# A decoder layer on one core: per-head scores on 32 rows of the array, and projections without a bias product

## The reference

```
x = x + attn(layernorm(x))        # 16 heads of 32, rope on q and k, causal, bias on q, k, v and on the output
x = x + xattn(layernorm(x), ctx)  # 16 heads of 32, int8 fake-quantised q and output projections,
                                  # plain k and v from ctx with biases, no mask
x = x + moe(layernorm(x))         # 64 experts, top 8 of a softmax, at most 128 rows per expert, width 192
```

## Time and profile before

| what | value |
|---|---|
| time, median of 3 runs | 1941.37 us |
| profiled execution, its span | 1982.1 us |
| PE busy | 1741.5 us, 88% |
| PE weight loads busy | 1208.5 us, 61% |
| DVE busy | 1257.8 us, 63% |
| ACT busy | 928.6 us, 47% |
| POOL busy | 547.6 us, 28% |
| mean granted PE clock | 0.953 |

### The profile page before, as it was taken

One profiled execution on the slowest core, in us unless ns is written; L12 is line 12 of the kernel. 1 busy time (PEld: TensorE's weight loads), 2 busy tenths in 40 slices (PEclk: granted clock), 3 DMA queues, 4 the chain that ended last, 5 costly groups with the idle time before them and its releaser, 6 DMA issues.

```text
span 1982.1 us, 31956 instructions
## 1 busy us (share of the span) xinstructions
PE 1741.5 (88%) x9128; PEld 1208.5 (61%) x9128; DVE 1257.8 (63%) x3136; ACT 928.6 (47%) x2737; POOL 547.6 (28%) x564
## 2 busy tenths in 40 slices
PE   3999999999999999999999999999957778778774
PEld 2676666666666666666666666666634455445453
DVE  7677777777777777777777777777743333333332
ACT  3465544555555445555554455555523333332331
POOL 4023223223332232223322322233222221212122
PEclk8999999999999999999999999999968988988887
DMA  9712121111101000000010000000075999998883
GB/s 355 254 45 95 72 81 73 68 60 57 41 25 38 27 21 21 21 21 21 21 34 24 26 21 21 21 21 21 22 197 157 233 237 224 230 229 219 226 216 43
DMA packets 119232, 190.29 MB, mean 96 GB/s; under 512 B 34373, under 2 KB 51141, under 8 KB 119208
## 3 DMA queue, kind: packets, MB, share of 16 engines
q1 hardware_dynamic: 89512, 154.20, 24.5%
q0 software_dynamic: 29696, 35.80, 9.4%
HBM read 126.61 MB, written 119.96 MB: 124 GB/s over the span
## 4 chain that ended last, share of the span: by engine, by line
PE 54%; DMA 22%; DVE 10%; issue 6%; ACT 5%; another core or an unknown queue 2%; POOL 0%; POOLq 0%; SPq 0%; DVEq 0%; ACTq 0%
PE bank L402 28%; DMA out<-x,slots 20%; PE bank L413 7%; PE bank L422 4%; PE bank L408 3%; PE bank L385 3%; ACT probs L678 3%; PE bank L430 3%; DVE kbd L1000 2%; PE bank L438 2%; DVE small L894 1%; PE bank L565 1%; DVE probs L1060 1%; PE bank L390 1%
## 5 line engine op out<-in xcount | busy, mean ns | idle before, releaser
L1224 POOL DMA_INDIRECT routed<-row,slots x256 | 268.2, 1047 | 284.9 <-DVE chosen_before L929 211.4
L678 ACT ACTIVATE probs<-bank,small 128x128 f32<-128x128 f32 x1024 | 322.3, 422 | 47.9 <-DVE small L894 47.2
L1216 POOL TENSOR_TENSOR small<-small,half 128x1 f32<-128x1 f32 x96 | 53.9, 562 | 628.3 <-DVE small L849 628.3
L894 DVE TENSOR_REDUCE small<-bank 128x4 f32<-128x512 f32 x256 | 171.2, 689 | 65.2 <-PE bank L416 47.1
L1304 POOL DMA_INDIRECT out<-x,slots x64 | 99.3, 1552 | 380.6 <-DVE slots L1176 265.4
L678 ACT ACTIVATION_READ_ACCUMULATOR probs<-bank,small 128x1 f32 x512 | 152.2, 301 | 0.0
L422 PEld LDWEIGHTS bank<-idf,probs 128*128 128x128 f32 x1024 | 119.2, 141 | 51.0 <-issue 28.0
L413 PE MATMUL bank<-kbd,qT 128*128 128x512 f32 x256 | 135.9, 612 | 6.7 <-DVE kbd L1000 6.7
L665 ACT ACTIVATE probsT<-bank 128x512 f32<-128x512 f32 x256 | 137.5, 636 | 6.1 <-PE bank L422 3.1
L422 PE MATMUL bank<-idf,probs 128*128 128x128 f32 x1024 | 138.3, 273 | 2.0 <-DVE probs L1060 1.4
L430 PEld LDWEIGHTS bank<-xv,probsT 128*128 128x128 f32 x1024 | 122.7, 193 | 11.1 <-issue 10.3
(11 more groups left out here) (249 smaller groups left out, 3982.4 us busy)
## 6 DMA issues: line engine op xcount, KB each, us to landing
w_gate_up<-in_w_gate SPq DMA_DIRECT2D x64, 384.0 KB
w_gate_up<-in_w_up SPq DMA_DIRECT2D x64, 384.0 KB
w_down<-in_w_down SPq DMA_DIRECT2D x64, 384.0 KB
routed<-empty_row SPq DMA_DIRECT2D x4, 4616.0 KB, 21.5
x_in<-in_x SPq DMA_DIRECT2D x32, 256.0 KB, 2.8
ctx_sb<-in_ctxT_in SPq DMA_DIRECT2D x32, 256.0 KB, 2.8
x_res<-in_x SPq DMA_DIRECT2D x32, 256.0 KB, 2.7
out<-x SPq DMA_DIRECT2D x32, 256.0 KB, 2.0
```

The costliest lines, as they stand in the source:

```text
L678: last = act.activation(probs[:, g, j * P:(j + 1) * P], bank[:, b, j * P:(j + 1) * P], ACT.Exp, bias=negmax[:, h:h + 1], **({"accum_out": ...
L894: dve.tensor_reduce(negmax[:, g * GH:(g + 1) * GH], bank[:, b, :].rearrange("p (j k) -> p j k", j=GH), AX_X, ALU.max, negate=True).then_in ...
L1224: pool.indirect_dma_start(routed, bass.IndirectOffsetOnAxis(ap=slots[:, k:k + 1], axis=0), row[:, :], None, bounds_check=SLOTS - 1, oob_is ...
```

## The change

Queries and keys stay in plain transposed tiles of 128 partitions x 4 x 128. A head sits on 32 of the 128 partitions, and its score product takes only these 32 rows of the array and 128 columns of keys. Head `4i + j` sits on row group `j` (32 rows) at place `i`; the four heads of one row group share a PSUM bank. For cross attention the sixteen products go round the four row groups and their four banks. For self attention two row groups go together in a pair (banks 2 and 6, later 0 and 4), after the mask product of each bank. Group numbers of `weigh`, `average` and `weigh_turned` now mean row groups; the value columns are permuted to suit, and so are the rows of the o weights on the host.

The zeroed tiles, the spreading copies of ACT and DVE and their zero fills go away. The 12-row bias product goes too. The biases are now added elsewhere: q in the DVE instruction that scales the queries, k in the DVE copy of the keys, xk in a new DVE copy of the cross keys (line 1031 of the kernel after), xv by a new POOL addition to `xv1`, v and o together by a new POOL addition to the residual tile `x_res`. q and k biases are roped and transposed once ahead of the first body, and the v bias goes once through the o projection there.

```diff
-            def project(b, hi, lo, name, first=0, end=1 + 3 * KT):
-
+            def project(b, hi, lo, name, first=0, end=3 * KT):
 
                 w_hi, w_lo = W[name]
-                steps = [(bias_of[:, BIASES.index(name), :], bias_rows[:, :])]
+                steps = []
...
-            def scores(b, g, q, kb, causal_mask, done):
-
-                last = pe.matmul(bank[:, b, :], q[:, g, :], kb[:, g, :, :].rearrange("p j t -> p (j t)"),
-                                 start=True, stop=not causal_mask)
+            def scores(banks, rows_of, q, keys, causal_mask, done):
+
                 if causal_mask:
-                    last = pe.matmul(bank[:, b, :], idb[:, :], mask_add[:, :].unsqueeze(1).to_broadcast([P, GH, P]),
-                                     start=False, stop=True)
-                last.then_inc(done, 1)
+                    for b in banks:
+                        pe.matmul(bank[:, b, :], idb[:, :], mask_add[:, :].unsqueeze(1).to_broadcast([P, GH, P]),
+                                  start=True, stop=False)
+                for i in range(NG):
+                    for b, j in zip(banks, rows_of):
+                        own = slice(j * DH, (j + 1) * DH)
+                        last = pe.matmul(bank[:, b, i * P:(i + 1) * P], q[own, i, :], keys[own, i, :],
+                                         start=not causal_mask, stop=not causal_mask or i == NG - 1)
+                        if i == NG - 1:
+                            last.then_inc(done, 1)
...
-                    for g in range(NG):
-                        scores(CROSS_BANK[g], g, cqT, xkbd, False, p_xs)
+                    scores(CROSS_BANK, range(GH), cqT, xkT, False, p_xs)
...
-                    if with_self and g < 2:
-                        if g == 0:
-                            until(pe, d_qT, cur)
-                            until(pe, a_kbd, cur)
-                            until(pe, d_kbd, cur)
-                        scores(SELF_BANK[g], g, qT, kbd, True, p_s)
+                    if with_self and g == 0:
+                        until(pe, d_qT, cur)
+                        until(pe, d_kT, cur)
+                        scores(SELF_BANK[0:2], (0, 1), qT, kT, True, p_s)
...
-                    if g == 0 and with_self:
-                        scores(0, 2, qT, kbd, True, p_s)
+                    if g == 1 and with_self:
+                        scores(SELF_BANK[2:4], (2, 3), qT, kT, True, p_s)
                 if with_self:
                     turn(1, xk_sb, p_xkT)
-                    scores(4, 3, qT, kbd, True, p_s)
                     project(3, cT_hi, cT_lo, "xv").then_inc(p_xv, 1)
...
                 pe.wait_ge(s_wTr, 3)
+                project(4, attT_hi, attT_lo, "o").then_inc(s_wT, 1)
...
-                    until(dve, s_x_res, prev * 16)
+                    until(dve, g_res, prev)
...
-                    for j in (2, 3):
-                        last = dve.tensor_copy(kbd[j * DH:(j + 1) * DH, :, j, :],
-                                               bank[j * DH:(j + 1) * DH, 6, :].rearrange("p (g t) -> p g t", g=NG))
-                    last.then_inc(d_kbd, 1)
+                    dve.tensor_tensor(wide_a[:, 0:D], bank[:, 6, :], k_biasT[:, :], ALU.add).then_inc(d_kT, 1)
...
+                if with_self:
+                    until(dve, p_xkT, cur)
+                    dve.tensor_tensor(xkT, bank[:, 1, :].rearrange("p (g t) -> p g t", g=NG),
+                                      xk_bias[:, :].unsqueeze(2).to_broadcast([P, NG, P]), ALU.add).then_inc(d_xkT, 1)
                 if with_self:
                     norm_probs(2, cur)
                     norm_probs(3, cur)
...
-            dve.wait_ge(s_wprep, 5)
-            dve.wait_ge(s_wT, 3)
-            dve.wait_ge(s_zeroed, 2)
+            dve.wait_ge(s_wprep, 6)
+            dve.wait_ge(s_wT, 4)
+            dve.tensor_tensor(att_bias[:, :], bank[:, 4, :], xatt[:, :], ALU.add).then_inc(s_wprep, 1)
...
+                if with_self:
+                    if not with_cross:
+                        pool.wait_ge(s_wprep, 7)
+                    until(pool, s_x_res, cur * 16)
+                    pool.tensor_tensor(x_res[:, :], x_res[:, :], att_bias[:, :], ALU.add).then_inc(g_res, 1)
                 if with_before:
                     scatter(prev - 1)
+                if with_self:
+                    until(pool, a_xv, cur)
+                    pool.tensor_tensor(xv1[:, :, 0:DH], xv1[:, :, 0:DH],
+                                       xv_bias[:, :].rearrange("p (h d) -> p h d", h=H), ALU.add).then_inc(g_xvb, 1)
```

More of the change, by code:

```diff
@@ L249, in layer @@
             w_dn.append(sb(f"w_down{k}", [FP, 2, D]))
-        tiles = [t[:, :, :, :].rearrange("p g j t -> p (g j t)") for t in (kbd, xkbd)] + \
+        tiles = [t[:, :] for t in (wide_a, wide_b)] + \
                 [t[:, :, :].rearrange("p g n -> p (g n)") for t in (probs, probsT)]
@@ L425, in weigh @@
             def weigh(b, g, vals, done):
-                for j in range(GH):
-                    h = g * GH + j
-                    at = (h % 8) * VW
-                    last = pe.matmul(bank[:, b, at:at + VW], probsT[:, g, j * P:(j + 1) * P], vals[:, h, :],
+                for i in range(NG):
+                    h = i * GH + g
+                    at = (g % 2 * NG + i) * VW
+                    last = pe.matmul(bank[:, b, at:at + VW], probsT[:, g, i * P:(i + 1) * P], vals[:, h, :],
                                      start=True, stop=True)
@@ L434, in weigh_turned @@
             def weigh_turned(b, g):
-                for j in range(GH):
-                    h = g * GH + j
-                    last = pe.matmul(bank[j * DH:(j + 1) * DH, b, g * P:(g + 1) * P], v_sb[:, h * DH:(h + 1) * DH],
-                                     probsT[:, g, j * P:(j + 1) * P], start=True, stop=True)
+                for i in range(NG):
+                    h = i * GH + g
+                    last = pe.matmul(bank[i * DH:(i + 1) * DH, b, g * P:(g + 1) * P], v_sb[:, h * DH:(h + 1) * DH],
+                                     probsT[:, g, i * P:(i + 1) * P], start=True, stop=True)
                 last.then_inc(p_pv, 1)
@@ L665, in copy @@
                 act.activation(dst, src, ACT.Copy).then_inc(done, 1)
-            def spread_keys(b, kb, heads):
-                for j in heads:
-                    last = act.activation(kb[j * DH:(j + 1) * DH, :, j, :],
-                                          bank[j * DH:(j + 1) * DH, b, :].rearrange("p (g t) -> p g t", g=NG), ACT.Copy)
-                return last
             def exponentials(b, g, done, total=None):
@@ L1120, in _ @@
             dve.wait_ge(s_const, 16 * N_CONST)
[L1121 to L1126 removed]
+            for src, at, crossed in ((x1, 0, xk_sb), (x2, D, xn2)):
+                turn_pairs(src[:, :].rearrange("p (h d) -> p h d", d=DH), roped[:, at:at + D], crossed[:, :], d_wchain)
+                chain[0] += 3
+            dve.wait_ge(d_wchain, chain[0])
+            dve.tensor_tensor(roped[:, 0:D], roped[:, 0:D], xk_sb[:, :], ALU.add)
+            dve.tensor_tensor(roped[:, D:2 * D], roped[:, D:2 * D], xn2[:, :], ALU.add).then_inc(s_wprep, 1)
+            spread_v = v_bias[:, :].unsqueeze(2).to_broadcast([P, KT, P])
+            chained(dve.tensor_copy(attT_hi[:, :, :], spread_v))
+            chained(dve.tensor_tensor(attT_lo[:, :, :], spread_v, attT_hi[:, :, :].bitcast(F32), ALU.subtract))
+            dve.wait_ge(s_biasT, 2)
+            dve.tensor_scalar(q_biasT[:, :], bank[:, 2, :], SCALE, None, ALU.mult)
+            dve.tensor_copy(k_biasT[:, :], bank[:, 3, :]).then_inc(s_wprep, 1)
             next_xT(1)
```

130 lines of the change are left out of this document (63 added, 67 removed).

## The result

The changed kernel takes 1959.28 us (median of 5 runs, 1954.79 to 1979.12) beside 1940.60 us for the kernel before (5 runs). The ratio is 1.0117, 95% interval 1.0080 to 1.0154: slower by 1.2%, where 1905 us and faster was forecast. The profiled execution is the one of 1979.12 us.

A forecast was written before the change was run, and what follows sets the result against it. PE was taken as the bound only up to its meetings with DVE or ACT. From 1941 us, 31 bodies at 1.4 us took off 43 and setup added 5: 1903, rounded to 1905, range 1860 to 1985.

The forecast's parts named there:

- its rival: PE's wait ahead of the second quantised tile: 3.4 us lets the clock fall, costing 1.5 per body; about 1945 us, chance 0.2.
- a gain of 43: Loop total: 1.4 us saved per body over 31 bodies, 43 us.
- The bias products: Six projections: dropping each 12-row product saves 0.63 us, 3.8 us of PE per body, of which q keeps 0.20.
- The walk: One body: 0.1 to 0.2 us gained ahead of the third self maximum, 1.05 behind the second tile's quantisation; 1.2 in all.
- I carry the difference over unscaled: Whole kernel: gain and cost worked out in the 1982.1 us profiled span applied to the 1941.37 median, giving 1903.
- Scores on row groups: Attention scores: loads and streams overlap, so cross scores take 1.5 us (3.44 before) and a self pair 1.8 (2.2 before).
- row groups load one after another: Score products: cross takes 3.9 us, a pair 2.6, losing 1.6 per body; about 1995 us, chance 0.25.
- The faster scores are spent: Third self maximum: starts at 24.6 us into the body against 24.7 before, so quicker scores bring almost nothing there.
- The waits: PE idle some 2 us ahead of the first cross transposition and 3.4 ahead of the second quantised tile.
- the text's own measure: Second quantised tile: the mechanism is wrong if PE still waits under 1 us there.
- The pause on DVE: Second average: its 1.45 us pause moves where DVE waits anyway, a body gains 2.9; near 1860 us, chance 0.23.
- Setup: Ahead of the first body: v bias through the o projection and roped biases cost +5 us, bounded by 2 and 10.

The follow-up runs named there:

- before_1scatter: The kernel before with one of the eight scatters of routed rows per body instead of eight: 0.9710 of the kernel before.
- nobias_again: The kernel before without its 12-row bias products, biases left out of the result, all scatters kept: 0.9527 of the kernel before.
- fill_both: The changed kernel with eight xv products moved behind the cross scores and twelve unread products ahead of the second quantised tile: 0.9670 of the kernel before.
- rows_filled: `fill_both` with a 12-row product put back ahead of each projection: 1.0060 of the kernel before.
- filler8b: The changed kernel with eight unread 512-column products behind the cross scores, in the wait for the first exponentials: 1.0253 of the kernel before.
- before_again: The kernel before, unchanged, run once more for a second trace: 0.9997 of the kernel before, 2013 us.
- xv_split_1scatter: The changed kernel with eight of twelve xv products moved behind the cross scores, and one scatter of eight: 0.9606 of the kernel before.

## Why the prediction was wrong

The step that failed is the clock in the new waits. The forecast put it at nothing, and its rival priced a fall at 1.5 us, in the longer wait alone. The runs showed falls behind the shorter wait in 24 of 31 bodies, 3.5 us a body on average (43.5 for 40.0). That is some 109 us where a gain of 43 was added up. With the clock held a body takes 2.5 us less than the 42.5 estimated below for the kernel before, a gain of 78; with 109 lost and 5 for the setup that makes 36 us more, and the profiled execution took 38 more than the median of before (an estimate). The rest of this section takes the terms one by one.

**The bias products: right price, wrong walk.** The price held in xv: twelve products end 2.79 us behind the transposition, against 3.40 for thirteen behind a mask (`before_1scatter`). Over the bodies PE's busy time fell by 3.3 to 3.5 us each, where the text had 3.6 to 3.8. The walk let only 0.1 to 0.2 of the gain through ahead of the third maximum and 1.05 behind the second tile. It took that second tile as tied to a DVE chain of 8.45 us with the pause of 1.45 in it, and a PE wait of 0.9. But that pause was the mark of held-up signals in that one execution, whose span of 1982 stood 41 us above the median (its chip is not on record). A median of 1941 leaves 42.5 us a body if what is ahead of and behind the bodies took as long as in the traces, an estimate. A body without held-up signals (`before_1scatter`) takes 42.4 and has no PE wait there. From there to `nobias_again` the second tile moves from 31.9 to 30.3 behind the start of the body and the body shrinks from 42.4 to 39.7: 2.7 us. Of these, 1.05 came behind the tile, exactly the step's number, and 1.65 ahead of it, where the step had next to nothing. "I carry the difference over unscaled" failed too: a sum worked out inside a disturbed execution was laid on the median of runs that by this estimate were undisturbed. This erred towards too small a gain, so it did not turn the sign.

**Scores on row groups: right, and worth nothing.** 1.17 us for cross scores (1.5 taken, though its own working gives 1.3) and 1.5 with masks for a pair (1.8 taken). The rival "row groups load one after another" is refuted: an instruction costs 0.035 us on four row groups, well under its limit of 0.08, and 0.07 on the two of a pair. The Trainium skill ("TensorE: Matmul & The Clock Gate", Part 3) says that such loads overlap, and the trace agrees. "The faster scores are spent" was right too: `fill_both` against `nobias_again` gives 0.967 and 0.953, and `rows_filled` 1.006.

**The waits: one right, one half as long.** The wait of "some 2 us" ahead of the first cross transposition is 1.94. The one of 3.4 ahead of the second tile is 1.68 in the bodies at full clock, where the tile comes at 30.6 (33.0 forecast). In the 13 longest bodies PE does not wait there at all, so by the text's own measure (under 1 us there) the mechanism failed in those. The same DVE instruction was to come every 42.6 us: it comes at 40.0 where the clock holds.

**The clock: the step that turned the sign.** The rival named the fall of the clock, with chance 0.2, but only for the longer wait and at 1.5 us a body, a price read from a few products in the experts. (Its sum is 1949, not 1945.) The clock fell behind the shorter wait, in 13 of 31 bodies for long, and cost 6 to 7.4 us in each; in 11 more it cost 1 to 4. What I argued against it, a loop at granted clock 1.00, was taken over from other waits. In seven bodies of that trace PE waited 1.8 to 1.9 us ahead of the second tile and the clock stayed at 1.00 behind it. So the length of a wait alone does not tell, and a wait at a new place has no row of before. And the price of a fall is not the few products behind the wait, but all that PE does until the clock is back: here transpositions, 33-column weighings and 32-row scores, for up to 21 us. Had the clock held, the change would have given some 0.967, or 1876 us, an estimate from `fill_both`: more gain than the forecast of 1905.

**The pause on DVE.** The rival expected the pause to move off the path. It did go, with the chip and with the scatters. That `fill_both` and the changed kernel's own profiled run have none, and runs on the slower chips have it whatever the kernel, speaks against the place of the code as its cause.

**Setup** was +5.1 us (first body's x1 at 84.44, before at 79.36), as taken.

What stays open: why the same wait of 1.94 us let the clock fall in 24 bodies and not in 7; how a scatter holds up PE's signals (its landing, or its writing of descriptors), and why on some chips only. No run took these apart. Also untried is a kernel with block-diagonal keys and the biases moved off PE, which these runs point to; `nobias_again` bounds it at 0.953 plus what the moved additions cost.

## What to carry to other kernels

A change that shortens TensorE's work can open a wait, and the wait can cost more than the work did. Before you shorten it, find where the first wait will open, and put other work of its own or unread products into it. Price a fall not by the next few products but by all that runs until the clock is back. In these bodies 17 to 21 us at the lower level cost 6 to 7.4. That is under half, since the later wait of 1.68 us is gone in them. And where a profiled execution stands 2% above the median, look first for what in it is not in the others, such as waits that no work explains, and leave it out of the sum.

## What the runs showed of the hardware

- A wait of 1.94 us between score products and transpositions was followed by a fall of the granted clock in 24 bodies of 31, the same code each time: for long in 13 and for less in 11; in 7 it stayed at 1.00. In one of the 13, PE was busy 10.26 of 10.30 us behind it with 128-column transpositions, 32-row scores, 33-column products and four mask products (granted clock 0.53), and the clock did not rise; it rose during or behind the twelve products of xv.
- Waits at another place did less. Ahead of the second tile, the clock stayed at 1.00 behind seven waits of 1.8 to 1.9 us in the kernel before, and behind 20 of 26 waits of some 2.0 to 2.8 us in `before_again`. Behind waits of 3.37 us there (`xv_split_1scatter`) it fell in every body.
- Sixteen unread products of 128 columns in the wait did as much as eight of 512 (1.0229 and 1.0253).
- 32 float32 score instructions on four row groups and four banks take 1.17 us, 0.035 us each; 16 on two row groups take 1.16 us, 0.07 each. The first 512-column product behind the 32 ends 0.43 us after them and the next 0.24 later (`fill_both`), so the change of mode of some 0.2 us is there too.
- A product of 12 rows ahead of each projection costs 2.7 us a body for six (42.4 to 39.7, `before_1scatter` and `nobias_again`), and in `rows_filled` 2.2 (42.4 for 40.2).
- On chips where the kernel before took 1987 to 2016 us, receivers of PE's results started late while the eight scatters went out, by 1.6 and 5.4 us in one body of `filler8b`; with one scatter the kernel before gained 2.9%. With all scatters, where it took 1938 us, `fill_both` showed none of it.
